# Cross-attention with a mixture-of-experts layer: attention slots and value pieces rearranged, tiles placed on multiples of 128 bytes, the hand-over to the experts changed

## The chip, the cores and the metric

The kernel runs on one core of a Trainium2 chip. The metric is the device time of one execution in microseconds: three runs took 1840.67, 1841.35 and 1837.13 us, median 1840.67. The profiled execution took 1836.25 us.

## The reference, cut to what matters

```python
x = x + tanh(g_xattn) * attention(layernorm(x), ctx, mask)      # x: 8 x 224 x 512, ctx: 8 x 750 x 512
    # Q, K, V = projections, 16 heads of 32; rotary embedding on Q and K
    # softmax(Q K^T / sqrt(32), masked) V, then W_o
xn = layernorm(x)
affinity = softmax(xn @ gate_w.T)                # 8 experts
gating, idx = top_k(affinity per batch and expert, k = 56)
h = silu(x_in @ w_gate) * (x_in @ w_up)          # x_in = xn[idx], 448 rows for each expert, inner width 2048
out.at[idx].add(gating * (h @ w_down))
x = x + tanh(g_ffn) * out
```

Everything is float32. Products that need it are made of three fp32r matmuls (high*high, high*low, low*high), whose low part is the value minus its rounded high part.

## The kernel before, in words

Three stages follow one another, each a block that all engines leave together.

**project_context** makes the keys and values of all 8 batches. `keys` runs 24 matmuls of 376 columns for each group of heads (two column halves n, four slices c of the contraction, three products); `c_hi`, `c_lo` are streamed and `w_hi`, `w_lo` are the weights. `values` does the reverse with 512 columns.

**attend** is written out for 8 batches b and in each for 16 slots t, one for each head. The order is fixed by hand: each engine's `body` has its own list by slot, and semaphores tie the lists. In slot t TensorE turns the softmax numerators of head t (`turn_rows`, three tiles of four transposes from `sm` into the two banks `t_ps`; tile n waits until tile n-2 has been copied out), and makes the scores of head t + 3 (`scores`, two row halves, four matmuls). VectorE masks the scores of head t + 3 (`mask_scores`, two instructions), ScalarE exponentiates those of head t + 2 (`exp`, two instructions). The three tiles are copied to `e_t` by either engine (`empty`); `DVE_TILES` says which go to VectorE. Four heads are a quad. The product with the values (`values`) runs for the quad before, four heads side by side in 32 columns of the array each, in three pieces of two chunks of keys, one piece in each slot with t % 4 not zero, behind the first tile. Other work hangs on slots: the next batch's queries (`turn_x`, `project_q`), the last batch's output projection, layer norm and gate logits (`project_out`, `turn_x2`, `logits`). Softmax sums pass through `invert` (VectorE), `spread_parts` (GpSimd), `turn_parts` (TensorE), `copy_parts` (ScalarE) to `normalise` (VectorE). In `end` the last batch is finished, and `rounds` on VectorE picks the top 56 of 224.

SP's queue carries all plain loads. In `end` it loads the first four tiles of expert weights `w_raw` as soon as the last scores are made.

**experts** loops over 8 experts. A weight tile (128x1024) is loaded to `w_raw`, split by ScalarE (`w_hi`) and VectorE (`w_lo`). `gate_up` runs 24 matmuls for each of 16 tiles (streamed `xs_hi`, `xs_lo`), `down` 24 for each of 8 tiles (streamed `h_hi`, `h_lo`), all with 448 columns. Before the first expert: TensorE brings gates and indices into PSUM (`turned`), VectorE casts the indices (`idx_t`), GpSimd copies one expert's to `gather_i` and issues four gathers of 112 rows into `xg`, TensorE turns them once all four have landed, and ScalarE and VectorE split them (`split_x`). VectorE's and ScalarE's splits of the first three weight tiles stand between the indices and `split_x`.

The start addresses in a partition, modulo 128 bytes, as the allocation gives them:

| tile | before | after |
|---|---|---|
| `xs_hi`, `xs_lo`, `h_lo` (streamed) | 0 | 0 |
| `h_hi` (streamed) | 64 | 0 |
| `ws_hi`, `ws_lo` (expert weights) | 64 | 0 |
| `c_hi`, `c_lo` (streamed in `keys`) | 32, slice pitch 3008 | 0, slice pitch 3072 |
| `w_hi`, `w_lo` (weights in `keys`) | 0 | 0 |
| `ks`, `qs`, `xT`, `e_t` | 64 | 0 |

With the pitch of 3008 and halves that begin 1504 bytes apart, the streamed rows of `keys` in its second half begin at 0, 64, 0, 64 modulo 128 for c = 0 to 3.

Of the kernel before, what the change touches and what calls it, by code (L numbers as in the profile page):

```python
# [7 lines left out]
F32R = mybir.dt.float32r  # L8
# [6 lines left out]
ds = bass.ds  # L15
# [27 lines left out]
LEAD = 3  # L43
WAYS = 32
# [25 lines left out]
F_XT, F_Q, F_USES = 0, 2, 4  # L70

# [46 lines left out]
def program(nc, ctxT, x, maskq, wk, wv, wq, wo, gatew, gx, gf, wstream, consts, rotations, out):  # L118
# [5 lines left out]
    with ExitStack() as top:  # L124
# [15 lines left out]
        w_in = [sem(f"w_in{j}") for j in range(NRAW)]  # L140

        with ExitStack() as mid:
# [8 lines left out]
            with ExitStack() as late:  # L151
                sb(late, "below", [P, IC * SLOTS - E_OVER * (KC // 2) * PAIR])
                w_raw = [sb(late, f"w_raw{j}", [P, UNIT]) for j in range(NRAW)]
# [5 lines left out]
                x_t=sb(mid, "x_t", [QP, QC, D]), xn=sb(mid, "xn", [QP, QC, D]), xT=sb(mid, "xT", [P, 2, 2 * S]),  # L159
                q_rot=sb(mid, "q_rot", [P, NG, S]), q_cos=sb(mid, "q_cos", [P, NG, S]),   # L160
                qs=sb(mid, "qs", [3 * WAYS, H, S], F32R), mq=sb(mid, "mq", [QP, QC, SK]),
                stats=sb(mid, "stats", [QP, QC, 6]), mv=sb(mid, "mv", [QP, 2, QC, 2]), var=sb(mid, "var", [QP, 2, QC]),
                rstd=sb(mid, "rstd", [QP, 2, QC]), minus_half=sb(mid, "minus_half", [QP, QC]), wq=sb(mid, "wq_sb", [P, DC, D]),
# [7 lines left out]

            project_context(nc, sem, sb, ps, both, ctxT, wk, wv, wq, x, maskq, gx, gf, consts, rotations, kd, vd, cst, gains)
            attend(nc, sem, sb, ps, both, x, maskq, wo, gatew, kd, vd, xn_rows, out, cst, ident,
                   cos, sin, gains, gate_all, row_all, wstream, w_raw, w_in)
        experts(nc, sem, sb, ps, w_raw, w_in, wstream, xn_rows, out_rows, cst, ident, gains, gate_all, row_all)


def project_context(nc, sem, sb, ps, both, ctxT, wk, wv, wq, x, maskq, gx, gf, consts, rotations, kd, vd, cst, gains):

    with ExitStack() as st:  # L180
        wraw, c_raw, k_split, v_out = both.wraw, both.c_raw, both.k_split, both.v_out
        w_hi = sb(st, "w_hi", [P, 2, DC, D], F32R)
        w_lo = sb(st, "w_lo", [P, 2, DC, D], F32R)
        graw = sb(st, "graw", [P, 2])
# [3 lines left out]
        c_lo = [sb(st, f"c_lo{j}", [P, DC, SK], F32R) for j in range(2)]  # L188
# [402 lines left out]
VPART = KC // (HG - 1)  # L591
XLEAD = 2
DVE_TILES = {0: (0, 1, 2), 1: (1,), 2: (1,), 6: (1, 2), 7: (0, 1), 8: (0,), 10: (2,), 11: (1,), 12: (1,), 13: (0,), 14: (0,), 15: (1,)}
# [11 lines left out]
def attend(nc, sem, sb, ps, both, x, maskq, wo, gatew, kd, vd, xn_rows, out, cst, ident,  # L605
           cos, sin, gains, gate_all, row_all, wstream, w_raw, w_in):

    with ExitStack() as st:
# [8 lines left out]
        sm = sb(st, "sm", [QP, SR, QC, SK])  # L617
        least, sums = sb(st, "least", [QP, KSLOTS, QC]), sb(st, "sums", [QP, 2, QC, HG])
# [67 lines left out]
        with nc.Block() as block:  # L686
            @block.sync
            def _(sp):
# [63 lines left out]
                def end():  # L752
                    load_res(B - 1)
                    hold(m_made, NS * B)
                    for u in range(NRAW):
                        sp.dma_start(w_raw[u][:], wstream[u]).then_inc(w_in[u], 16)
# [981 lines left out]
```

## Time and profile before

| | us |
|---|---|
| median of three runs | 1840.67 |
| profiled execution | 1836.25 |
| its span, first to last instruction | 1834.4 |
| attention, steady batch | 65.3 |
| last scores to the first expert matmul | 795 to 860.5 |
| experts, from there to the end | 974 |

Columns of the rows below: a timeline row has start, duration, engine, line, operation, `out<-in`, the shape and the count, then how long the engine was idle before it and what ended that. TensorE's matmuls overlap, so how fast they follow is read from one start to the next. A plain fp32 matmul is recorded as two instructions.

### The profile page before, as it was taken

To read this page: it belongs to the slowest core of one execution; us is meant where nothing else is said; L and a number is where in the kernel's file an instruction comes from. 1 tells how busy PE (TensorE), PEld (TensorE's weight loads), DVE (VectorE), ACT (ScalarE), POOL (GpSimd) and SP (SyncE) were. 2 spreads that over 40 slices of the span, in tenths; PEclk is the share of its full clock that TensorE was granted. 3 is DMA by queue.
4 is the path that set the end of the run, shared out by engine and by line. 5 is a ranking of instruction groups with operands and counts; after the bars stand their busy time and mean duration, and the time that the engine had idled before them with its cause. 6 is when DMAs were issued, how large, how long until landed. Compare 5 with 4: busy or idle time off the path is not lost.

```text
span 1834.4 us, 28481 instructions
## 1 busy us (share of the span) xinstructions
PE 1740.8 (95%) x10502; PEld 1545.1 (84%) x10502; DVE 1038.9 (57%) x1786; ACT 839.2 (46%) x1482; POOL 235.4 (13%) x302
## 2 busy tenths in 40 slices
PE   7999999899999999983999999999999999999995
PEld 6898998677777877753999999999999999999995
DVE  6666667777887787754544535435445354453541
ACT  3223225777776877742433434424344243343430
POOL 0000002131231232122000102002020020010101
PEclk9999999999999999995999999999999999999998
DMA  6544547756755755523333535335343252353421
GB/s 242 224 173 186 189 156 220 182 126 153 178 147 135 183 150 134 141 87 96 115 104 103 150 109 143 103 103 151 106 121 127 106 149 104 101 150 109 124 92 20
DMA packets 76301, 251.90 MB, mean 137 GB/s; under 512 B 10784, under 2 KB 10784, under 8 KB 74928
## 3 DMA queue, kind: packets, MB, share of 16 engines
q1 hardware_dynamic: 64208, 216.55, 38.3%
q0 software_dynamic: 12000, 34.12, 7.9%
q8 instruction: 57, 0.93, 0.2%
q14 instruction: 36, 0.29, 0.1%
HBM read 188.01 MB, written 51.61 MB: 131 GB/s over the span
## 4 chain that ended last, share of the span: by engine, by line
PE 52%; POOL 1%; DVE 0%; issue 0%; DMA 0%; DVEq 0%; ACT 0%; POOLq 0%
PE gu_ps L1624 11%; PE gu_ps L1623 11%; PE gu_ps L1622 11%; PE y_ps L1641 6%; PE y_ps L1640 6%; PE y_ps L1639 6%; PE y_ps L1650 1%; PE gu_ps L1608 1%; POOL out L1482 0%; DMA xg<-xn_rows,gather_i 0%; POOL gather_i L1469 0%; POOL xg L1472 0%; DVE xs_lo L1557 0%; DVE y_cols L1584 0%; PE gu_ps L1668 0%
## 5 line engine op out<-in xcount | busy, mean ns | idle before, releaser
L1622 PE MATMUL gu_ps<-xs_hi,ws_hi 128*128 128x448 f32 x1024 | 370.3, 362 | 3.0 <-DVE xs_lo L1557 3.0
L1624 PE MATMUL gu_ps<-xs_hi,ws_lo 128*128 128x448 f32 x1024 | 371.9, 363 | 0.0
L1623 PE MATMUL gu_ps<-xs_lo,ws_hi 128*128 128x448 f32 x1024 | 371.8, 363 | 0.0
L1552 DVE TENSOR_TENSOR ws_lo<-w_raw,ws_hi 128x1024 fp32r<-128x1024 f32 x192 | 235.2, 1226 | 189.3 <-ACT ws_hi L1502 188.3
L1502 ACT ACTIVATE ws_hi<-w_raw 128x1024 fp32r<-128x1024 f32 x192 | 201.5, 1051 | 163.7 <-PE y_ps L1641 150.6
L1298 PEld LDWEIGHTS t_ps<-cst,sm 112*125 112x125 f32 x1536 | 205.0, 190 | 68.6 <-issue 29.3
L990 DVE CUSTOM_DVE_ANT_0 sm<-m_ps,mq 112x752 f32<-112x752 f32 x256 | 229.7, 935 | 34.2 <-PE m_ps L1282 33.8
L1298 PE MATMUL t_ps<-cst,sm 112*125 112x112 f32 x1536 | 233.3, 281 | 15.0 <-DVE e_t L998 11.3
L880 ACT ACTIVATE sm<-sm,least 112x752 f32<-112x752 f32 x256 | 234.7, 919 | 13.7 <-DVE least L990 12.7
L1622 PEld LDWEIGHTS gu_ps<-xs_hi,ws_hi 128*128 128x128 f32 x1024 | 192.0, 187 | 16.9 <-issue 3.3
L1623 PEld LDWEIGHTS gu_ps<-xs_lo,ws_hi 128*128 128x128 f32 x1024 | 192.7, 188 | 14.6
L1624 PEld LDWEIGHTS gu_ps<-xs_hi,ws_lo 128*128 128x128 f32 x1024 | 192.6, 188 | 10.4
L1523 ACT ACTIVATE silu<-gu_ps 128x448 f32<-128x448 f32 x128 | 69.8, 545 | 274.2 <-PE gu_ps L1624 272.2
L1641 PE MATMUL y_ps<-h_hi,ws_lo 128*128 128x448 f32 x512 | 187.8, 367 | 0.0
L1640 PE MATMUL y_ps<-h_lo,ws_hi 128*128 128x448 f32 x512 | 187.6, 367 | 0.0
L1639 PE MATMUL y_ps<-h_hi,ws_hi 128*128 128x448 f32 x512 | 187.4, 366 | 0.0
L887 ACT ACTIVATE e_t<-t_ps 125x448 f32<-125x448 f32 x256 | 137.4, 543 | 107.6 <-PE t_ps L1298 106.2
L1571 DVE TENSOR_TENSOR hid<-silu,gu_ps 128x448 f32<-128x448 f32 x128 | 79.6, 622 | 188.2 <-ACT silu L1523 188.2
L1482 POOL DMA_INDIRECT out<-y_sb,scatter_i x32 | 52.4, 1637 | 860.5 <-DVE y_sb L1562 853.2
L1574 DVE TENSOR_TENSOR h_lo<-hid,h_hi 128x448 fp32r<-128x448 f32 x128 | 80.0, 625 | 82.5 <-ACT h_hi L1525 81.8
L1282 PE MATMUL m_ps<-ks,qs 96*112 96x376 f32 x512 | 120.0, 355 | 5.0 <-PEq L227 1.7
L1525 ACT ACTIVATE h_hi<-hid 128x448 fp32r<-128x448 f32 x128 | 74.0, 578 | 88.0 <-DVE hid L1571 88.0
(153 smaller groups left out, 2438.6 us busy)
## 6 DMA issues: line engine op xcount, KB each, us to landing
w_raw<-wstream SPq DMA_DIRECT2D x192, 512.0 KB, 3.5
ks<-k_split SPq DMA_DIRECT2D x192, 188.0 KB, 5.4
k_split<-k_split SPq DMA_DIRECT2D x32, 752.0 KB, 3.4
v_rows<-v_out SPq DMA_DIRECT2D x16, 750.0 KB
vs<-v_rows SPq DMA_DIRECT2D x16, 750.0 KB
c_raw<-ctxT SPq DMA_DIRECT2D x7, 1500.0 KB, 13.0
qs<-q_hi POOLq DMA_DIRECT2D x64, 112.0 KB, 5.1
mq_raw<-maskq SPq DMA_DIRECT2D x7, 656.2 KB, 10.9
```

What stands on the lines that cost most here:

```text
L880: nc.scalar.activation(rows, rows, ACT.Exp, bias=least[:, h % KSLOTS, qc:qc + 1], scale=-1.0, accum_out=sums[:, h // HG % 2, qc, h % HG:h ...
L887: nc.scalar.activation(e_t[h % (2 * HG)][:, pc], t_ps[tile_of(b, h, pc) % 2][0:KP, 0:PAIR], ACT.Copy).then_inc(t_act, 1)
L990: nc.vector.tensor_tensor_reduce(sm[:, h % SR, qc].rearrange("p (a n) -> p a n", a=2), m_ps[qc][0:QP, :, 0:KN], mq[:, qc].rearrange("p (a ...
L1298: mm = nc.tensor.transpose(t_ps[n % 2][0:KP, a:a + QP], sm[:, h % SR, qc, c * KP:c * KP + KP], ident[0:QP, 0:QP])
L1502: nc.scalar.activation(w_hi[s][:], w_raw[s][:], ACT.Copy).then_inc(whi_done, 1)
L1552: nc.vector.tensor_tensor(w_lo[s][:], w_raw[s][:], w_hi[s][:], ALU.subtract).then_inc(wlo_done[s], 1)
L1622: nc.tensor.matmul(o, w_hi[s][:, w], xs_hi[:, c], start=(c == 0), stop=False)
L1623: nc.tensor.matmul(o, w_hi[s][:, w], xs_lo[:, c], start=False, stop=False)
L1624: mm = nc.tensor.matmul(o, w_lo[s][:, w], xs_hi[:, c], start=False, stop=(c == DC - 1))
L1639: nc.tensor.matmul(o, w_hi[s][:, w], h_hi[:, i], start=(i == 0), stop=False)
L1640: nc.tensor.matmul(o, w_hi[s][:, w], h_lo[:, i], start=False, stop=False)
L1641: mm = nc.tensor.matmul(o, w_lo[s][:, w], h_hi[:, i], start=False, stop=(i == IC - 1))
```

## The change

In `attend`, the three value pieces of a quad become one or two, put at the end of a slot: all six chunks in slots 1 and 7, four and two in 10 and 11, four and two in 13 and 15. The four score matmuls of a slot are parted, two ahead of tile 1 and two behind it. ScalarE makes both exponentials behind tile 0. `DVE_TILES` gives VectorE 15 tiles of 48 and not 16, in other slots. Most side work moves by a slot or two. The copies of the weight tiles to `w_hi` and `w_lo` for the first three units move from the start of `experts` to the end of `attend`.

In `experts`, VectorE writes `gather_i` for expert 0 straight from PSUM, ahead of the gates; each of the four gathers has its own semaphore, TensorE turns each when it has landed, the first matmuls wait for `xs_lo` slice by slice, and SP loads nothing further until the first gathers have landed. Tiles are moved and padded as in the table above.

```diff
-DVE_TILES = {0: (0, 1, 2), 1: (1,), 2: (1,), 6: (1, 2), 7: (0, 1), 8: (0,), 10: (2,), 11: (1,), 12: (1,), 13: (0,), 14: (0,), 15: (1,)}
+V_CHUNKS = {1: (0, KC), 7: (0, KC), 10: (0, 4), 11: (4, KC), 13: (0, 4), 15: (4, KC)}
+DVE_TILES = {0: (0,), 1: (0, 1), 2: (1,), 3: (1,), 4: (0, 1), 6: (1,), 8: (0,), 9: (1,), 11: (0, 1), 12: (0,), 14: (1,), 15: (0,)}
...
-        c_hi = [sb(st, f"c_hi{j}", [P, DC, SK], F32R) for j in range(2)]
+        c_hi = [sb(st, f"c_hi{j}", [P, DC, SK + LINE // 2], F32R) for j in range(2)]
...
# attend, ScalarE
-                            if pc < QC:
-                                next_exp(pc)
+                            if pc == 0:
+                                for qc in range(QC):
+                                    next_exp(qc)
...
                 def end():
                     copy_parts(B - 1, NG - 1)
+                    for u in range(LEAD):
+                        act.wait_ge(first.w_in[u], 16)
+                        nc.scalar.activation(first.w_hi[u][:], first.w_raw[u][:], ACT.Copy).then_inc(first.whi_done, 1)
                     x2_columns(B - 1, 0)
...
# attend, VectorE, end
                     norm_2(b)
+                    low_w(0)
                     dve.wait_ge(rest_made, R_USES * b + R_XNT + 2)
                     nc.vector.tensor_copy(xT[:, 1], m_ps[1][:, 1, 0:2 * S]).then_inc(rest_free, 1)
+                    low_w(1)
+                    low_w(2)
                     logits(b)
...
# attend, TensorE, a slot
                         turn_rows(b, t, 0)
-                        if t % HG:
-                            last_values()
+                        next_scores(0)
                         turn_rows(b, t, 1)
-                        next_scores(0)
                         next_scores(1)
                         turn_rows(b, t, 2)
...
+                        if t in V_CHUNKS:
+                            last_values()
...
# attend, TensorE, end
-                    for part in range(HG - 1):
-                        values(b, NG - 1, part)
+                    values(b, NG - 1, (0, KC))
...
# experts, SP
+                for g in range(RG):
+                    hold(gathered[g], 16)
                 for u in range(NRAW, NU):
                     load(0, u)
...
# experts, GpSimd
+                    if isinstance(e, int) and e == 0:
+                        hold(gidx_done, 1)
...
# experts, VectorE
                 dve.wait_ge(turned, 1)
+                nc.vector.tensor_copy(gather_i, gu_ps[0][0:RP, RG * E:2 * RG * E].rearrange("p (g e) -> p g e", g=RG)[:, :, 0:1]
+                                      .rearrange("p g o -> p (g o)")).then_inc(gidx_done, 1)
...
-                for u in range(LEAD):
-                    split_w(0, u)
                 split_x(0)
...
# experts, TensorE
-                    pe.wait_ge(gathered, 16 * RG * (e + 1))
-                    for c in range(DC):
-                        for g in range(RG):
+                    for g in range(RG):
+                        pe.wait_ge(gathered[g], 16 * (e + 1))
+                        for c in range(DC):
...
-                    if u == 0:
-                        pe.wait_ge(xlo_done, DC * (e + 1))
...
+                            if u == 0 and k == 0:
+                                pe.wait_ge(xlo_done, DC * e + c + 1)
```

TensorE's instructions in program order, slot 7 of a middle batch, before. `t_ps` are the transposes, `m_ps` the scores, `o_ps<-e_t,vs` a piece of values, `w_ps<-wo_sb,cx` the output projection; a count is of matmuls in the program, and the piece stands behind the first tile.

```order
L1298 MATMUL t_ps<-cst,sm 125x112 x4
L1322 MATMUL o_ps<-e_t,vs 32x224 x8
L1298 MATMUL t_ps<-cst,sm 125x112 x4
L1282 MATMUL m_ps<-ks,qs 112x376 x4
L1298 MATMUL t_ps<-cst,sm 125x112 x4
L1222 MATMUL w_ps<-wo_sb,cx 112x512 x2
```

The same slot in the changed kernel:

```order
L1330 MATMUL t_ps<-cst,sm 125x112 x4
L1314 MATMUL m_ps<-ks,qs 112x376 x2
L1330 MATMUL t_ps<-cst,sm 125x112 x4
L1314 MATMUL m_ps<-ks,qs 112x376 x2
L1330 MATMUL t_ps<-cst,sm 125x112 x4
L1254 MATMUL w_ps<-wo_sb,cx 112x512 x2
L1354 MATMUL o_ps<-e_t,vs 32x224 x24
```

Slots 5 and 6 have lost their pieces of 8, one piece of 24 closes slot 7, and the scores are parted.

VectorE from the last layer norm to the gate logits, at the end of `attend`, after the change (`ws_lo` are low parts of the first weight tiles, `lg` the logits):

```order
L999 TENSOR_SCALAR xn<-x_res,mv,rstd 112x512 x2
L1121 TENSOR_TENSOR ws_lo<-w_raw,ws_hi 128x1024
L1207 COPY xT<-m_ps 128x448
L1121 TENSOR_TENSOR ws_lo<-w_raw,ws_hi 128x1024 x2
L1085 COPY lg<-w_ps 112x16
```

VectorE from the end of `attend` into `experts`, before the change; the three `ws_lo` stand behind the indices and ahead of the split of the gathered rows:

```order
L1089 TENSOR_SCALAR gate_all<-top_v,cst 64x56
L1090 TENSOR_SCALAR row_all<-top_i,cst 64x56
L686 UNCONDITIONAL_BRANCH
L1547 UNCONDITIONAL_BRANCH
L1588 TENSOR_SCALAR gate_t<-gu_ps,gains 112x4x8
L1590 CAST idx_t<-gu_ps 112x4x8
L1552 TENSOR_TENSOR ws_lo<-w_raw,ws_hi 128x1024 x3
L1557 TENSOR_TENSOR xs_lo<-gu_ps,xs_hi 128x448 x4
```

And after; the index copy of expert 0 (`both_i` holds `gather_i`) has come from GpSimd and is first:

```order
L1113 TENSOR_SCALAR gate_all<-top_v,cst 64x56
L1114 TENSOR_SCALAR row_all<-top_i,cst 64x56
L706 UNCONDITIONAL_BRANCH
L1580 UNCONDITIONAL_BRANCH
L1621 CAST both_i<-gu_ps 112x4
L1623 TENSOR_SCALAR gate_t<-gu_ps,gains 112x4x8
L1625 CAST idx_t<-gu_ps 112x4x8
L1590 TENSOR_TENSOR xs_lo<-gu_ps,xs_hi 128x448 x4
```

Nothing of VectorE's own stands between the indices and the split any more.

## Rows read from the trace of the kernel before

**Rows 1.** Busy time by stage: us, then PE, PEld, DVE, ACT, POOL, clock, DMA.

```profile
540.10:605.40 65.30, 62.65 (x538) 50.44 (x537) 52.14 (x125) 48.82 (x108) 17.07 (x27) 1.00 0.65 155
800.00:850.00 50.00, 22.54 (x168) 14.79 (x168) 22.71 (x75) 7.87 (x15) 11.92 (x11) 0.69 0.30 102
```

**Rows 2.** Timeline of TensorE in the last batch, a piece of values among others.

```profile
771.33 0.59 PE L1298 MATMUL t_ps<-cst,sm 112*125 112x112 f32 x4
771.85 0.96 PE L1322 MATMUL o_ps<-e_t,vs 125*32 125x224 f32 x16
...
773.20 0.92 PE L1282 MATMUL m_ps<-ks,qs 96*112 96x376 f32 x4
...
780.88 1.02 PE L1298 MATMUL t_ps<-cst,sm 112*125 112x112 f32 x8
...
781.67 0.91 PE L1282 MATMUL m_ps<-ks,qs 96*112 96x376 f32 x4
...
811.73 2.48 PE L1322 MATMUL o_ps<-e_t,vs 125*32 125x224 f32 x48
```

**Rows 3.** Waits of TensorE in three steady batches: total, times, longest.

```profile
PE t_ps L1298 <- DVE e_t L998: 4.2, 6, 0.8
```

**Rows 4.** Instruction groups in one steady batch: busy us, mean ns, idle before.

```profile
L880 ACT ACTIVATE sm<-sm,least 112x752 f32<-112x752 f32 x34 | 31.2, 920 | 1.2 <-DVE least L990 1.1
L990 DVE CUSTOM_DVE_ANT_0 sm<-m_ps,mq 112x752 f32<-112x752 f32 x33 | 29.6, 934 | 3.7 <-PE m_ps L1282 3.7
...
L887 ACT ACTIVATE e_t<-t_ps 125x448 f32<-125x448 f32 x32 | 17.3, 544 | 14.1 <-PE t_ps L1298 13.9
```

**Rows 5.** Timeline at the end of `attend`, last batch's gate logits.

```profile
809.02 1.86 SPq L756 DMA_DIRECT2D w_raw<-wstream  x4
...
822.79 0.54 ACT L857 ACTIVATE xT<-w_ps 128x448 f32<-128x448 f32 x1 [12.32 <-PE w_ps L1249]
823.09 3.11 POOL L795 TENSOR_SCALAR x2o<-x_res,flags_sb 112x512 f32<-112x512 f32 x2
823.17 0.62 DVE L1177 COPY xT<-m_ps 128x448 f32<-128x448 f32 x1 [1.46 <-PE m_ps L1249]
...
827.04 0.17 DVE L1061 COPY lg<-w_ps 112x16 f32<-112x16 f32 x1 [3.25 <-PE w_ps L1262]
```

**Rows 6.** Timeline at the start of `experts`, VectorE and GpSimd.

```profile
842.28 3.48 DVE L1552 TENSOR_TENSOR ws_lo<-w_raw,ws_hi 128x1024 fp32r<-128x1024 f32 x3
842.47 3.35 POOL L1469 COPY gather_i<-idx_t 112x4 uint32<-112x4 uint32 x1 [14.97 <-DVE idx_t L1590]
```

**Rows 7.** Chain of waits that ended last, in order of time: start, us, what.

```profile
846.71 1.05 POOL xg L1472
...
850.55 3.58 DMA xg<-xn_rows,gather_i
854.27 3.23 PE gu_ps L1608 x16
...
858.11 2.23 DVE xs_lo L1557 x4
860.47 0.71 PE gu_ps L1622
861.18 0.37 PE gu_ps L1623
```

**Rows 8.** Lines of the expert matmuls in 880:930 and 950:974: min/median/max ns, first and last start.

```profile
L1622 PE MATMUL gu_ps<-xs_hi,ws_hi x84: 360/360/360, 880.0 to 929.8; 128*128 128x448 f32 x84
...
L1639 PE MATMUL y_ps<-h_hi,ws_hi x40: 362/364/450, 950.1 to 974.0; 128*128 128x448 f32 x40
```

**Rows 9.** Timeline of `keys`, second half, first matmul of slices c = 0 to 2.

```profile
242.15 0.33 PE L526 MATMUL k_ps<-c_hi,w_hi 128*128 128x376 f32 x1
...
242.67 0.33 PE L526 MATMUL k_ps<-c_hi,w_hi 128*128 128x376 f32 x1
...
243.18 0.33 PE L526 MATMUL k_ps<-c_hi,w_hi 128*128 128x376 f32 x1
```

More of the change, by code:

```diff
@@ L43 @@
 LEAD = 3
+LINE = 32
+TOP_EDGE, MID_EDGE = 16, 16
+BEFORE = 2 * (B // 2) * D + DC * SLOTS + 2 * SLOTS
+FIRST = BEFORE + 3 * LINE
 WAYS = 32
@@ L70 @@
 F_XT, F_Q, F_USES = 0, 2, 4
+@dataclass
+class First:
+    w_raw: object
+    w_hi: object
+    w_lo: object
+    w_in: object
+    whi_done: object
+    wlo_done: object
 @dataclass
@@ L139, in program @@
         gains = sb(top, "gains", [P, 2])
-        w_in = [sem(f"w_in{j}") for j in range(NRAW)]
+        sb(top, "top_edge", [P, TOP_EDGE])
         with ExitStack() as mid:
@@ L151, in program @@
             with ExitStack() as late:
-                sb(late, "below", [P, IC * SLOTS - E_OVER * (KC // 2) * PAIR])
-                w_raw = [sb(late, f"w_raw{j}", [P, UNIT]) for j in range(NRAW)]
+                sb(late, "below", [P, FIRST - E_OVER * (KC // 2) * PAIR])
+                first = First(
+                    w_raw=[sb(late, f"w_raw{j}", [P, UNIT]) for j in range(NRAW)],
+                    w_hi=[sb(late, f"ws_hi{j}", [P, UNIT], F32R) for j in range(NRAW)],
+                    w_lo=[sb(late, f"ws_lo{j}", [P, UNIT], F32R) for j in range(NRAW)],
+                    w_in=[sem(f"w_in{j}") for j in range(NRAW)], whi_done=sem("whi_done"),
+                    wlo_done=[sem(f"wlo_done{j}") for j in range(NRAW)])
             ks = sb(mid, "ks", [3 * WAYS, KSLOTS, SK], F32R)
@@ L183, in project_context @@
         w_lo = sb(st, "w_lo", [P, 2, DC, D], F32R)
+        c_hi = [sb(st, f"c_hi{j}", [P, DC, SK + LINE // 2], F32R) for j in range(2)]
+        c_lo = [sb(st, f"c_lo{j}", [P, DC, SK + LINE // 2], F32R) for j in range(2)]
         graw = sb(st, "graw", [P, 2])
@@ L605, in attend @@
 def attend(nc, sem, sb, ps, both, x, maskq, wo, gatew, kd, vd, xn_rows, out, cst, ident,
[L606 removed]
+           cos, sin, gains, gate_all, row_all, wstream, first):
     with ExitStack() as st:
@@ L617, in attend @@
         sm = sb(st, "sm", [QP, SR, QC, SK])
+        e_t = [sb(st, f"e_t{j}", [KP, KC // 2, PAIR]) for j in range(E_OVER, 2 * HG)] + both.e_t
         least, sums = sb(st, "least", [QP, KSLOTS, QC]), sb(st, "sums", [QP, 2, QC, HG])
         parts, spread = sb(st, "parts", [QP, 2, QC * HG]), sb(st, "spread", [QP, 2, QC, P])
-        e_t = [sb(st, f"e_t{j}", [KP, KC // 2, PAIR]) for j in range(E_OVER, 2 * HG)] + both.e_t
         c_r, cx = sb(st, "c_r", [P, S]), sb(st, "cx", [P, NG, S])
@@ L1092, in _, with low_w @@
                 SOFT = 4
+                def low_w(u):
+                    dve.wait_ge(first.whi_done, u + 1)
+                    nc.vector.tensor_tensor(first.w_lo[u][:], first.w_raw[u][:], first.w_hi[u][:], ALU.subtract).then_inc(first.wlo_done[u], 1)
                 def start():
@@ L1307, in turn_parts, with values @@
                     mm.then_inc(r_made, 1)
-                def values(b, q, part):
+                def values(b, q, chunks):
                     a, quad = q // 2, q % 2
-                    if part == 0:
+                    if chunks[0] == 0:
                         if quad == 0:
@@ L1317, in values @@
                             pe.wait_ge(s_, v_)
-                    for c in range(VPART * part, VPART * part + VPART):
+                    for c in range(*chunks):
                         for r in range(HG):
@@ L1423, in experts @@
         gidx_done, sidx_done = sem("gidx_done"), sem("sidx_done")
-        gathered, x_turned, xhi_done, xlo_done = sem("gathered"), sem("x_turned"), sem("xhi_done"), sem("xlo_done")
+        gathered, x_turned, xhi_done, xlo_done = [sem(f"gathered{g}") for g in range(RG)], sem("x_turned"), sem("xhi_done"), sem("xlo_done")
         silu_done, hid_done = sem("silu_done"), [sem(f"hid_done{j}") for j in range(2)]
@@ L1591, in _ @@
                                       gu_ps[0][0:RP, RG * E:2 * RG * E].rearrange("p (g e) -> p g e", g=RG)).then_inc(idx_ready, 1)
-                for u in range(LEAD):
-                    split_w(0, u)
                 split_x(0)
```

123 lines of the change are left out of this document (61 added, 62 removed).

## The prediction

> **What bounds the kernel now.** I read the busy time by stage first, then the timeline of each stage, the waits and the chain. In a steady batch of the attention TensorE is busy for 62.65 of 65.3 us, VectorE for 52.1, ScalarE for 48.8; between the attention and the experts TensorE works for less than half of 50 us, at a mean clock of 0.69 [rows 1]. In the attention TensorE sets the pace, and its 2.65 us of idle time in a batch are short waits for a copy out of `t_ps` [rows 3]. In the gap everything is one chain: last layer norm, gate logits, top-k on VectorE, indices, gathers, transposes, split, first matmul at 860.47 [rows 5 to 7]. From there TensorE has work without a break to the end. So the change is read at three places: the attention's slots, the gap, and the pace of the matmuls.
>
> **The attention's slots: fewer pieces.** Four transposes, a piece of 16 instructions (8 matmuls) and four transposes take from 771.33 to 773.20, 1.87 us; eight transposes with no piece between them take from 780.88 to 781.67, 0.79 us [rows 2]. A piece costs 1.08 us. The last quad's single piece of 48 takes 2.48 us [rows 2]; three of 16 would be 3.24. So each piece that is left out saves (3.24 - 2.48) / 2 = 0.38 us; since the end of a matmul is modelled I take 0.35. Before there are 9 pieces in the first batch, 12 in each of seven, and one at the end: 94. Now 5, 6 each, and one: 48. Of the 46 saved, the 4 of batch 0 count for nothing, because that batch has no output projection and its copies hold it anyway. 42 x 0.35 = **-14.7 us**.
>
> Parting the scores costs nothing that I can find: the four matmuls and their neighbours are the same, and one more change between transposes and scores replaces one that was there beside a piece. Bounds: 0, or, if each change costs what a piece's edges do beyond its work (0.35), 128 slots x 0.35 = +45. The second is far off, as eight transposes with scores behind them show no such gap [rows 2]; I take 0 and +4 as its end. It also gives each tile more time to be copied out, which could take away waits.
>
> What is late next: the pieces no longer fill every slot. A slot with neither piece nor projection holds 12 transposes and four scores, some 2.1 us of TensorE (0.79 + 0.4 + 0.9 [rows 2]), but ScalarE needs two exponentials of 0.92 and two or three copies of 0.54, 2.9 to 3.5 us [rows 4]. Such slots were 0, 8 and 12; now they are 0, 8, 9 and 12. In slots 0, 8, 9, 12 ScalarE's lists come to 3.8, 3.3, 2.9 and 3.3 us (with the copies of sums and `xT`), TensorE's to 2.65, 2.25, 2.4 and 2.25 (small transposes included): 3.7 us of waits in a batch, if nothing is carried over from slot to slot. But exponentials run two heads ahead, and in slots 5 to 7, where TensorE has an output projection or six chunks on top of its 2.1 us, the others catch up. The same reckoning for the old order gives about 4 (with VectorE's three copies in slot 0), where 2.65 were idle. I take the waits as unchanged: 0, between -1.3 us a batch (half of them go, as a piece no longer waits for `copy_parts` in slots 9 and 13) and +1.05 (3.7 against 2.65): -10 to +8 in all.
>
> **The end of the attention.** In the last batch the last piece of quad 2 now ends slot 15, right ahead of `turn_parts`, which needs its `normalise`: one exposed multiply and its hand-over, **+0.6**. ScalarE's three copies of weights: it has been idle for 12.32 us at 822.79, the loads are issued at 809.02 to 810.9, and three copies of 1 us fit: 0 [rows 5]. VectorE's first `ws_lo` (1.16 us: three in 3.48 [rows 6]) follows the layer norm, which ends at 821.7, and the copy to `xT` before began at 823.17: hidden but for nothing to spare. The other two, 2.3 us, follow that copy, 823.8 to 826.1, and the logits' copy comes at 827.04: hidden [rows 5]. But GpSimd's `x2o` runs from 823.09 for 3.11 us [rows 5]. In rows 6 a small GpSimd copy of 16 numbers lasts 3.35 us, exactly as long as VectorE's three `ws_lo` beside it. If here VectorE is the one that waits, for each of two instructions of 1.55 us, the logits' copy slips to about 828.7. So 0 to +1.6; I take **+0.5**.
>
> The Trainium skill says on this, in "SBUF — State Buffer", section "Who interferes with whom", that a VectorE instruction with two SBUF inputs and a GpSimd instruction that reads SBUF exclude each other for the whole instruction, and whichever comes first blocks the other. By that rule the trace agrees with its 3.35 us, and both ends of this term and the gain of the next one follow from it.
>
> **The start of the experts.** GpSimd's copy of indices (842.47, 3.35 us) goes. The cast on VectorE at 842.02 lasts 0.2, and the same 0.85 us lie from its end to the first gather (845.8 to 846.71): it is issued at 843.15, **-3.55** [rows 6, 7]. Four gathers follow at the same spacing; the last lands at 854.13 - 3.55 = 850.6 [rows 7]. All 16 transposes were behind it, 3.23 us; now 12 are done, and four are left, 0.8 us: **-2.4**. The first matmul waited for all four `xs_lo` (2.23 us), now for the first, 0.56: **-1.7** [rows 7]. A slice's matmuls at the low clock take three times 0.37 us and a split 0.56, so the later slices aren't waited for. Sum -7.65. Three loads of 0.5 MB no longer share the time of the gathers; worth nothing to -0.5. Against it, TensorE may spend longer at the low of its two clocks (1.2 of 2.4 GHz): now some nine matmuls at 0.37 for 0.20, which is 1.5 us; twice that is the end. The gap in all: -7.65 + 0.6 + 0.5 = **-6.5**, -8.5 to -3.5.
>
> **The pace of the fp32r matmuls.** `gate_up`, streaming at 0 modulo 128 with weights at 64: 84 of one line from 880.0 to 929.8, three lines in turn, 49.8 / 249 = 0.200 us. `down`, where two of three stream `h_hi` at 64: 23.9 / 117 = 0.204 [rows 8]. If the offset makes the difference, aligning wins 0.004 x 1536 = 6 us. In `keys` the weights are at 0; slice c = 0 streams at 0 and takes 0.52 us for three matmuls of 376, slice c = 1 at 64 and takes 0.51 [rows 9]. There, alignment shows no gain at all. The 0.004 may as well come from `down` changing its accumulator every three matmuls. For `keys`, `values` and `scores`, 1856 matmuls, I allow 0 to -5 by the same spread of 0.003. On the other side, where both streams begin at 0 the slice was 0.01 slower; 0.003 x 3072 matmuls of `gate_up` would be +9. The bounds are +9 and -11; I take **-5**, nearest to the row of `down`.
>
> The Trainium skill's page "SBUF — State Buffer", section "Specifications (TRN2)", gives lines of 16 bytes. All offsets here were multiples of 32, so by that rule this term is 0 and the sum 5 us less gain; rows 9 agree with it, rows 8 leave it open.
>
> **Sum.** 1836.25 - 14.7 - 6.5 - 5 = 1810.0 for a profiled execution. The three runs of before lie 1 to 5 us above the profiled one, their median 4.4; I add 3: **1813 us**.
>
> **Rivals.** (a) The attention gives the gain back: 3.7 us of waits in a batch for 2.65, +8, and dearer changes between scores and tiles, +4: -2.7 in the attention, 1825 to 1829. For it speak ScalarE's full short slots, against it that its total is 48.8 of 65.3 [rows 1]. (b) Slower than before: no slot hides another's excess. Then VectorE's slot 4 (two masks 1.87, two copies 1.24, `normalise`, and the rotation and sum of the queries, of some 2.5: 5.9 us against TensorE's 3.8) and slot 13 (+0.7) join the 3.7: 6.5 us of waits in place of 2.65, +31 in eight batches, with no gain from alignment: 1836.25 - 14.7 - 6.5 + 31 = 1846, as a median 1849. It decides from 3.4 us of further waits in a batch. Against it: the old order by the same count would have idled for more than 6. (c) The offsets rule the matmul: at the low clock a matmul of 448 columns takes 0.37 us, twice 0.187, while at the high clock it takes 0.200 [rows 7, 8]. If full alignment removed that 0.0135 from 4608 matmuls, -62: about 1755. Against it rows 9, though 376 columns are no multiple of 32. The Trainium skill ("TensorE: Matmul & The Clock Gate", section "Wait — 56ns, not 53.3ns?") has 2.5 ns over the columns' own time for bf16, 0.189 here; by that it would be -51. No fp32r row of this trace reaches it. (d) Streams and weights at the same offset hinder one another: +9 for -5, 1827.
>
> **Chances.** Within 0.3% (5.5 us) of before can't be told from no change. Forecast 0.63; (a) 0.18; (b) 0.07; (c) 0.05; (d) 0.07. The forecast, (c), most of (a) and (d) are faster: 0.87; what spills over from (a), (b) and (d) into no change 0.07; slower 0.06. The forecast's own range is 1800 to 1824. With (a) and (d) taken in, 1798 to 1831; (b) and (c) lie outside.
>
> **What would show it.** Steady batches of about 63.4 us with 6 groups of value instructions; PE's idle time near 2.65 in each. If it exceeds 3.7, (a). First gather about 1.2 us after the index matmuls end at 841.97, not 4.7; transposes in four groups; first expert matmul some 12 us after those matmuls begin and not 19. `down` at 0.200 and `gate_up` still at 0.200. The forecast is wrong if the batch stays at 65, or if either pace moves by more than 0.004.

## The result and the profile after

The changed kernel takes 1846.14 us, median of 7 runs (1842.28 to 1855.62), against 1839.95 for the kernel before in 7 runs beside it (1837.13 to 1842.3): ratio of the runs 1.0047, interval 1.0032 to 1.0062 (the two medians alone give 1.0034). It is slower by a third to half a per cent; 1813 us had been forecast, and 1846 lies outside the range. The profiled execution took 1842.28 us with a span of 1840.5.

The starts of instructions in both traces cut the span into stages. The last two columns are for the version that the experiments lead to.

| stage, from and to | before | after | difference | e9_best |
|---|---|---|---|---|
| up to the first transpose of the attention | 295.7 | 296.4 | +0.7 | 296.5 |
| to the last transpose of a head's rows | 512.2 | 505.9 | -6.3 | 472.6 |
| to the first `gate_up` matmul | 52.6 | 47.1 | -5.5 | 47.3 |
| to the last `down` matmul | 951.9 | 968.8 | +16.9 | 947.0 |

The attention and the gap got shorter, the experts longer by more than both.

**The attention.** Two steady batches and the 50 us at the end of the attention, as [rows 1] (us, then busy time of PE, PEld, DVE, ACT, POOL, the granted clock, DMA):

```profile
482.90:547.10 64.20, 61.66 (x540) 51.09 (x536) 52.32 (x123) 48.60 (x108) 16.32 (x26) 0.97 0.65 157
547.15:611.90 64.75, 61.76 (x541) 51.04 (x537) 52.37 (x124) 48.69 (x108) 16.33 (x26) 0.97 0.68 160
...
800.00:850.00 50.00, 21.77 (x139) 13.71 (x138) 23.31 (x74) 7.01 (x14) 11.18 (x12) 0.67 0.28 94
```

From first transpose to first transpose the batches 1 to 6 take 64.0, 64.5, 64.3, 64.7, 64.8 and 65.3 us, so that none is more than 1.3 us shorter than the 65.3 of a steady batch before. What is new is the clock: 0.97, where [rows 1] has 1.00. TensorE's waits in three steady batches, as [rows 3]:

```profile
PE m_ps L1314 <- issue: 8.3, 3, 2.9
```

All the waits for a copy out of `t_ps` are gone, and one new wait stands in their place, once in each batch. "issue" says that no engine's work ended it. The timeline shows it in slot 1, ahead of the first scores of head 4 (start, us, engine, line, what):

```profile
549.78 0.60 PE L1330 MATMUL t_ps<-cst,sm 112*125 112x112 f32 x4
...
550.13 0.08 DVE L1014 DVE_READ_ACCUMULATOR2_ANT least<- 112x1 f32 x1
...
553.28 0.57 PE L1314 MATMUL m_ps<-ks,qs 96*112 96x376 f32 x2 [2.89 <-issue]
```

The mask of the head before was done at 550.2, so `m_ps` was free. Each DMA lands in 16 shares, and the trace records when: the last of the 48 shares of the keys for heads 4 and 5 landed at 553.19. The same batch cut at the wait, same columns:

```profile
547.15:550.40 3.25, 3.24 (x30) 3.06 (x26) 2.73 (x7) 3.09 (x8) 0.00 (x0) 1.00 1.04 227
550.40:553.25 2.85, 0.00 (x0) 0.00 (x1) 0.62 (x1) 2.03 (x5) 0.00 (x0) 1.00 1.05 227
553.25:555.00 1.75, 1.72 (x14) 1.75 (x15) 0.69 (x2) 0.00 (x0) 0.00 (x0) 1.00 1.04 159
555.00:558.40 3.40, 3.40 (x37) 1.86 (x39) 1.76 (x5) 1.09 (x2) 0.00 (x0) 0.51 1.01 205
558.40:611.90 53.50, 53.40 (x471) 44.37 (x461) 46.56 (x110) 42.48 (x94) 16.33 (x26) 1.00 0.60 150
```

Behind the 2.85 us without work the granted clock goes to 0.51, which is 1.2 of 2.4 GHz, for 3.4 us in which TensorE is busy throughout. That is another 1.7 us. The DMA shares of 1.01 to 1.05 say that the DMA engines are full up to 558.4. So the wait costs some 4.7 us in this batch, and without it the batch would be 60.0. Over the whole attention it is seven such waits, in the batches 1 to 7:

```profile
PE m_ps L1314 <- issue: 19.0, 7, 3.3
```

Six of them, in the batches 1 to 6, have 3.4 us at half the clock behind them. The one in batch 7, 2.43 us long, has not; a seventh such stretch begins at 797.4, 50 us behind it.

**The gap.** The end of the attention, as [rows 5], and the chain at the start of the experts, as [rows 6, 7]:

```profile
817.71 1.22 DVE L1121 TENSOR_TENSOR ws_lo<-w_raw,ws_hi 128x1024 fp32r<-128x1024 f32 x1
...
818.92 0.62 DVE L1207 COPY xT<-m_ps 128x448 f32<-128x448 f32 x1
819.17 4.26 POOL L815 TENSOR_SCALAR x2o<-x_res,flags_sb 112x512 f32<-112x512 f32 x2
819.46 2.63 DVE L1121 TENSOR_TENSOR ws_lo<-w_raw,ws_hi 128x1024 fp32r<-128x1024 f32 x2
...
822.79 0.17 DVE L1085 COPY lg<-w_ps 112x16 f32<-112x16 f32 x1 [0.70 <-PE w_ps L1294]
```

```profile
836.90 0.94 PE gu_ps L1701 x4
838.08 0.85 issue
838.93 1.04 POOL xg L1508
...
841.52 4.76 DMA xg<-xn_rows,both_i
846.33 1.77 PE gu_ps L1641 x8
848.13 0.55 ACT xs_hi L1542
848.70 0.64 DVE xs_lo L1590
849.47 0.71 PE gu_ps L1655
```

The logits' copy stands 3.87 us behind the start of the copy to `xT`, as before (823.17 to 827.04 in [rows 5]): the splits of weights hide there. GpSimd's `x2o` took 4.26 instead of 3.11 us, which nobody waits for. The first gather starts 1.1 us after the index matmuls' end, the first expert matmul 12.6 us after their start.

**The experts.** `gate_up` at 1000 to 1040 and 1120 to 1160, then `down` at 950 to 974, as [rows 8]; the first row is of before in the same stretch:

```profile
L1622 PE MATMUL gu_ps<-xs_hi,ws_hi x67: 360/360/360, 999.8 to 1039.4; 128*128 128x448 f32 x67
```

```profile
L1655 PE MATMUL gu_ps<-xs_hi,ws_hi x67: 362/365/369, 999.6 to 1039.8; 128*128 128x448 f32 x67
...
L1655 PE MATMUL gu_ps<-xs_hi,ws_hi x65: 368/368/368, 1120.0 to 1159.6; 128*128 128x448 f32 x65
...
L1672 PE MATMUL y_ps<-h_hi,ws_hi x37: 368/368/368, 949.8 to 972.2; 128*128 128x448 f32 x37
```

Before: 39.6 us for 66 x 3 matmuls, 0.200 us each. After: 40.2 for as many, 0.203, and in the second stretch 39.6 for 64 x 3, 0.206. Taken from start to start, the pace in the changed kernel is locked, that is, it stays at one value over hundreds of matmuls: 202.7 ns in one expert, 206.7 in the next, in turn, with `down` like `gate_up`. It changes within the first 96 matmuls of an expert. The means are 204.7 and 204.6 where before had 200.0 and 203.7. Over 3072 and 1536 matmuls that is 14.4 + 1.4 us, nearly all of the 16.9.

In `keys`, where [rows 9] had 0.52 and 0.51 us for three matmuls, both differences between the three starts are now 0.52. Over the whole stage the mean is 173.2 ns for 172.1, and that of `values` 232.6 for 232.1, about 1 us in all:

```profile
241.85 0.33 PE L546 MATMUL k_ps<-c_hi,w_hi 128*128 128x376 f32 x1
...
242.37 0.34 PE L546 MATMUL k_ps<-c_hi,w_hi 128*128 128x376 f32 x1
...
242.89 0.34 PE L546 MATMUL k_ps<-c_hi,w_hi 128*128 128x376 f32 x1
```

### The profile page after: what moved, and what is told of

Read it like the earlier page. It is cut to its first block, busy times and chain, and to the rows that moved or that the text cites. A ratio compares the mean times of both kernels' runs of the same rounds, so it can differ in the third digit from the quotient of the medians.

```text
span 1840.5 us, 28531 instructions
## 1 busy us (share of the span) xinstructions
PE 1753.1 (95%) x10502; PEld 1553.2 (84%) x10502; DVE 1040.7 (57%) x1779; ACT 837.8 (46%) x1490; POOL 226.6 (12%) x301
## 4 chain that ended last, share of the span: by engine, by line
PE 53%; POOL 0%; DMA 0%; issue 0%; DVE 0%; DVEq 0%; ACT 0%; POOLq 0%
PE gu_ps L1655 11%; PE gu_ps L1656 11%; PE gu_ps L1657 11%; PE y_ps L1672 6%; PE y_ps L1673 6%; PE y_ps L1674 6%; PE y_ps L1683 1%; PE gu_ps L1641 1%; POOL out L1518 0%; DMA xg<-xn_rows,both_i 0%; POOL xg L1508 0%; DVE y_cols L1617 0%; PE gu_ps L1701 0%; DVE y_sb L1595 0%; DVEq L1466 0%
## 5 line engine op out<-in xcount | busy, mean ns | idle before, releaser
L1655 PE MATMUL gu_ps<-xs_hi,ws_hi 128*128 128x448 f32 x1024 | 377.3, 368 | 1.4 <-DVE xs_lo L1590 1.4
L1657 PE MATMUL gu_ps<-xs_hi,ws_lo 128*128 128x448 f32 x1024 | 376.5, 368 | 0.0
L1656 PE MATMUL gu_ps<-xs_lo,ws_hi 128*128 128x448 f32 x1024 | 376.4, 368 | 0.0
L1330 PEld LDWEIGHTS t_ps<-cst,sm 112*125 112x125 f32 x1536 | 218.5, 190 | 31.8 <-issue 26.8
L1314 PE MATMUL m_ps<-ks,qs 96*112 96x376 f32 x512 | 150.7, 377 | 24.9 <-issue 19.0
L1518 POOL DMA_INDIRECT out<-y_sb,both_i x32 | 53.1, 1659 | 877.7 <-DVE y_sb L1595 870.4
```

What stands on the lines that cost most here:

```text
L1314: mm = nc.tensor.matmul(m_ps[qc][0:QP, n, 0:KN], qs[:, h, qc * QP:qc * QP + QP], ks[:, h % KSLOTS, n * KN:n * KN + KN], start=True, stop=True)
L1330: mm = nc.tensor.transpose(t_ps[n % 2][0:KP, a:a + QP], sm[:, h % SR, qc, c * KP:c * KP + KP], ident[0:QP, 0:QP])
L1655: nc.tensor.matmul(o, w_hi[s][:, w], xs_hi[:, c], start=(c == 0), stop=False)
L1656: nc.tensor.matmul(o, w_hi[s][:, w], xs_lo[:, c], start=False, stop=False)
L1657: mm = nc.tensor.matmul(o, w_lo[s][:, w], xs_hi[:, c], start=False, stop=(c == DC - 1))
```

## The experiments

Theory: two things cost what the rest gains. One is that streams and weights of the experts now start at the same offset modulo 128 bytes (before: `xs` 0, `h_hi` 64, `h_lo` 0, weights 64; now all 0). The other is the keys of head 4, which land late behind the values. Ratios are against the kernel before, which ran beside each; paces are means from start to start.

**e1_weights64.** The weights alone go back to 64.

```
-FIRST = BEFORE + 3 * LINE
+FIRST = BEFORE + 3 * LINE + LINE // 2
...
-        sb(st, "first_place", [P, 3 * NRAW, UNIT])
+        sb(st, "first_gap", [P, LINE // 2]), sb(st, "first_place", [P, 3 * NRAW, UNIT]), sb(st, "stream_gap", [P, LINE // 2])
```

> The changed kernel with the experts' weights (raw, high and low parts) 64 bytes further on, so that they start at 64 mod 128 as in the kernel before, while every streamed tile (xs, h) stays at 0. Theory 1 (a streamed row and the next weights at one offset mod 128 hinder one another): gate_up falls from 204.7 back to 200.0 ns a matmul (3072 of them, -14.4 us) and down, whose high part now differs from the weights too, from 204.6 to 200.0 (1536, -7.1 us): about 1825 us against 1846. Theory 2 (the slower pace comes from something else in the new build, such as where its code or its other tiles lie): both stay near 204.7 and the time stays within 3 us of 1846. Theory 3 (only the streams' own alignment counts, 200 wherever they are at 0): already refuted by the changed kernel unless the weights' offset matters, so it expects no change either.

Measured: 1823.75 us, ratio 0.9915 (0.9884 to 0.9946). `gate_up` and `down` both at 200.0 in every stretch. Theory 1 holds to the number, and `down` is faster than in either kernel.

```profile
L1655 PE MATMUL gu_ps<-xs_hi,ws_hi x67: 360/360/360, 1000.2 to 1039.8; 128*128 128x448 f32 x67
```

**e4_before0.** The converse: in the kernel before, everything of the experts at 0.

```
-                sb(late, "below", [P, IC * SLOTS - E_OVER * (KC // 2) * PAIR])
+                sb(late, "below", [P, 16 + IC * SLOTS - E_OVER * (KC // 2) * PAIR])
...
-        h_hi = sb(st, "h_hi", [P, IC, SLOTS], F32R)
+        sb(st, "gap", [P, 16]); h_hi = sb(st, "h_hi", [P, IC, SLOTS], F32R)
...
-        xg = sb(st, "xg", [RP, RG, D])
+        sb(st, "gap2", [P, 16]); xg = sb(st, "xg", [RP, RG, D])
```

> The kernel before with the experts' weights and the high part of h moved by 64 bytes, so that weights and streams all start at 0 mod 128 as in the changed kernel; nothing else is changed. Theory 1 (equal offsets hinder): gate_up slows from 200.0 to about 204.7 ns (+14.4 us), down goes from 203.7 to about 204.6 (+1.4): about 1855 us against 1840. Theory 2 (another part of the change made it): the pace stays 200.0 and 203.7 and the time within 3 us of 1840.

Measured: 1850.63 us, ratio 1.0065 (1.0048 to 1.0082), +12. `gate_up` 204.0, `down` 203.4. So 64 bytes more under the weights, with nothing else of the change, make the kernel before slow in the same way. (`h_hi` moves along by 64 bytes and `xs` by 128, which leaves `xs` at 0.) Here the pace is the same in every expert, another lock than that of the changed kernel.

**e2_map, e7_w32, e8_all64.** What about the other distances? In the first, buffer j of the weights starts at 32j (`UNIT + 8` wide) and chunk c of a stream at 32c (`SLOTS + 8` wide). The second is e1_weights64 with 8 floats ahead of the weights and 24 behind them instead of 16 and 16, the third e1_weights64 without `stream_gap`.

> One look for the pace alone. The four weight buffers of the experts start at 0, 32, 64 and 96 mod 128 (high and low part alike), and chunk c of the streamed tiles starts at 32c mod 128, so that each pair of offsets occurs in every expert. Theory 1 (equal offsets hinder): matmuls whose stream and weights have one offset take about 204.7 ns from start to start, those 64 bytes apart 200.0, with the quarter turns between or like one of the two. Theory 3 (a stream off a 128-byte line costs by itself): pace goes by the chunk alone, chunks 1 and 3 slowest. Theory 2 (neither): all combinations within 1 ns of each other. If the pace locks over a whole stretch, as the changed kernel's does (206.7 and 202.7 in turn from expert to expert), single combinations will not differ and only the stretch's mean will.

> One look for the pace: as the kernel with the weights at 64, but the weights at 32 mod 128 with the streams at 0. If what hinders is that both start in the same half of a 128-byte line, gate_up and down take more than 202 ns here; if only the very same offset does, 200.0; if 64 bytes apart is a special case, between 201 and 206, as the map of all pairs had (203.9 and 203.5).

> One look for the pace: weights and streams (xs, h) all at 64 mod 128. If the distance between the two is what counts, gate_up and down are as slow as with both at 0 (202.6 to 206.7, mean about 204.6); if a start at 64 of the weights by itself is what makes them fast, 200.0.

Measured, one execution each (1841.93, 1847.12, 1836.75 us), so that only the paces are compared:

| kernel | streams, weights (mod 128) | `gate_up`, ns | `down`, ns |
|---|---|---|---|
| before | `xs` 0, `h_hi` 64, `h_lo` 0; 64 | 200.0 | 203.7 |
| after | 0; 0 | 204.7 (202.7 or 206.7) | 204.6 |
| e4_before0 | 0; 0 | 204.0 | 203.4 |
| e8_all64 | 64; 64 | 203.2 (202.7 or 206.7) | 202.8 |
| e7_w32 | 0; 32 | 205.3 | 205.3 |
| e2_map | all pairs | 203.9 | 203.5 |
| e1_weights64 | 0; 64 | 200.0 | 200.0 |

The distance counts, not the offset itself: both at 64 is as slow, and locks at the same two paces, as both at 0. A distance of 32 is no better. Only 64 apart gives 200.0. The map did not tell single pairs apart: its pace too is locked over whole stretches, so that a pair's matmul depends on its neighbours. It shows only that a mixture isn't fast. No run moves one of the two operands by 128 bytes alone, so that the distance repeats every 128 bytes is how the offsets are written here and not shown.

**e3_keys.** The values are loaded behind the keys of heads 4 and 5.

```
-                        if t == 12 and not last:
+                        if t == 14 and not last:
                             load_v(b + 1, 0)
```

> The changed kernel with one DMA moved: the values of the next batch (750 KB) are loaded by SP behind the keys of its heads 4 and 5 instead of ahead of them (slot 14 of SP's order instead of 12). Theory A (the new 3.1 us wait of slot 1, at the first scores of head 4, is for keys that queue behind the values): the keys land 4 us or more earlier, the wait goes in the 6 or 7 batches that have it, about -18 us of the attention (ends 2 to 3 us a batch earlier), time about 1828. Theory B (the 16 DMA engines are saturated in this stretch whatever the order): the keys land at most 1 us earlier, the wait stays over 2 us, and the time within 6 us of 1846. Theory C (what is late next takes the place): the wait at head 4 goes, but another of over 1.5 us a batch shows in slots 2 to 7, for ACT's exp or head 6's keys.

Measured: 1814.97 us, ratio 0.9857 (0.9837 to 0.9877), 31 us less than the changed kernel, where 18 were expected. The keys of head 4 land 13.5 us ahead of the batch's first transpose, where they landed 6.0 after it. The wait is gone in all seven batches and nothing takes its place: a batch is 60.0 us. What I had left out was the clock: with the wait its half-speed stretch goes too. In batch 0 two waits of 3.6 and 3.8 us appeared, which end at 321.2 and 339.1 us, as keys land. The attention takes 482.5 us with them and 472.4 in the next version, which doesn't have them.

**e5_split.** The order stays, but the values are two DMAs.

```
-                    sp.dma_start(vs[a][:]..., vd[ds(b, 1), a]...).then_inc(vs_in[a], 16)
+                    for r in (slice(0, 112), slice(112, KP)):
+                        sp.dma_start(vs[a][r]..., vd[ds(b, 1), a, r]...).then_inc(vs_in[a], 16)
...
-                            pe.wait_ge(vs_in[a], 16 * b + 16)
+                            pe.wait_ge(vs_in[a], 32 * b + 32)
```

> The changed kernel with the order of its loads untouched, but each value load (125 rows, 750 KB) issued as two DMAs, of 112 and of 13 rows. In the trace of the changed kernel only 5 of the 16 shares of such a load land late (12 to 14 us after its issue, the other shares at once), and of the 16 shares of the keys for head 4 behind it 11 land within 7 us and 5 only after those. Theory A1 (125 rows are dealt out to 5 of the 16 DMA engines, and the keys' shares on those 5 wait behind them): with 112 rows dealt to 16, the keys of head 4 land before slot 1 although they still stand behind the values, the wait goes and the time falls to about 1815 to 1820, as where the keys were put first. Theory A2 (what counts is the 750 KB ahead of the keys, on whatever engines): the keys land less than 2 us earlier, the wait stays over 1.5 us a batch and the time stays above 1835.

Measured: 1806.81 us, ratio 0.9823 (0.9807 to 0.9839). Theory A1 holds: the keys still stand behind 750 KB and land in time. The landings of one batch's shares, in us from the issue of the values:

```
                      values: first, last         keys of heads 4 and 5: 33rd share, 34th, 48th
after (issued 534.75) 0.5; 5 shares at 13.1-14.1  7.0, 15.0, 18.4
e5_split (520.39)     1.0; 5.3                    7.1, 7.1, 7.9
```

A load of keys is three DMAs of 16 shares. In the changed kernel 33 shares, three times 11, are there after 7.0 us; the other 15, three times 5, come from 15.0 on, behind the 5 late shares of the values. Which engine carried a share isn't in the traces; that it is 11 engines and 5 is read from the counts. 125 rows have no larger divisor up to 16 than 5, while 112 go to all 16. The Trainium skill states this rule in "DMA: Bandwidth & Descriptors", section "Why a DMA increments its semaphore by 16 and not by 1": the outermost dimension is dealt to the largest number of engines up to 16 that divides it on both sides of the transfer, source and destination. The traces agree, with 5 late shares of 16.

The row of a whole batch of e5_split, as [rows 1], and the stretch that begins where the changed kernel fell to half speed, 5.0 us of work into the batch:

```profile
532.80:592.80 60.00, 59.90 (x540) 50.40 (x536) 52.39 (x125) 48.49 (x108) 16.34 (x26) 1.00 0.67 170
```

```profile
537.80:541.20 3.40, 3.40 (x57) 2.35 (x56) 1.51 (x5) 1.33 (x5) 0.00 (x0) 1.00 1.00 254
```

TensorE is busy for 59.90 of 60.00 us, and does 57 instructions in 3.4 us where it did 37. The DMA engines are nearly as full as in the changed kernel (1.00 for 1.01 in these rows), and the keys are there all the same: fullness was not what delayed them.

**e12_before_split.** The same edit in the kernel before.

> The kernel before with only its value loads issued as two DMAs (112 and 13 rows). In it the keys of head 4 land 4 us before they are needed, so the theory that says the value loads matter only by that wait expects no gain in the slots: 1838 within 3 us, and the whole 33 us between the changed kernel and its mended form is what the new arrangement of the slots lacked. Rival: the loads on 5 of 16 engines also delay others (stacked queries, mask, x) and the old waits of slots 8, 9, 12 and 13: then 5 us or more faster.

Measured: 1834.98 us, ratio 0.9979 (0.9967 to 0.999). The keys land 5.4 to 6.5 us before the first transpose instead of 0.2 to 1.9 after it, and the steady batches gain nothing: TensorE's waits in three of them are those of [rows 3], to a tenth:

```profile
PE t_ps L1298 <- DVE e_t L998: 4.3, 6, 0.8
```

So the 0.2% is not in the steady slots. One batch of the kernel before was not steady: in batch 1 the keys of heads 4 and 5 landed at 360.36 us, 7.0 after the first transpose. TensorE waited, and then ran at half its clock (a row of the timeline, and one by stage as in [rows 1]):

```profile
360.45 0.92 PE L1282 MATMUL m_ps<-ks,qs 96*112 96x376 f32 x4 [1.60 <-issue]
...
361.90:365.30 3.40, 3.40 (x25) 2.15 (x24) 1.11 (x4) 3.10 (x6) 0.00 (x0) 0.50 0.35 126
```

That batch took 68.2 us for 65.3, and takes 64.8 in e12_before_split. Batch 0 takes 59.5 there for 57.6, with a stretch at half the clock that it didn't have, and the attention as a whole 510.7 for 512.2. So apart from batch 1 the value loads cost something only where the new slots are.

**e11_gap_back and e9_best.** e9_best is the changed kernel with e5_split's and e1_weights64's edits. e11_gap_back is e9_best with the gap as before: splits at the start of `experts`, indices by GpSimd, one wait for all gathers and one for all low parts.

> The changed kernel with the values loaded as two DMAs (112 and 13 rows) and the experts' weights 64 bytes further on; the order of the loads is as in the changed kernel. If the two mendings add: 1806.8 (values in two, weights at 0) - 4608 matmuls x 4.65 ns = 21.4 us: 1785. Rival: the weights' shift costs something elsewhere (it gained 22 us alone but 20.5 beside the moved load, with longer half-clock stretches), then 1788 to 1792. In both cases gate_up and down at 200.0 ns, slots at 60.0 us a batch.

> As e9_best, but the part between attention and experts put back as in the kernel before: the first three weight units are split at the start of the experts, the first gather's indices are cast by GpSimd after all index work, the transposes wait for all four gathers, the first matmul for all four low parts. Nothing else changes, and the pace is locked at 200.0 ns in both. The prediction's own working of this edit: -7.65 us at the start of the experts, +0.6 and +0.5 given back at the end of the attention and on GpSimd: this kernel should take 5 to 8 us more than e9_best (about 1792). Rival: since TensorE's clock is at half speed in this stretch and comes back only some time after the work resumes, the saved idle time comes out otherwise: less than 3 or more than 9 us.

Measured: e9_best 1787.48 us, ratio 0.9719 (0.9706 to 0.9733); e11_gap_back 1794.99, ratio 0.9764 (0.9749 to 0.9779). The edit of the gap is worth 7.5 us; by the traces 54.1 - 47.3 = 6.8. The chain of e11_gap_back has GpSimd's copy of the indices back, 3.36 us where [rows 6] had 3.35:

```profile
804.64 3.36 POOL both_i L1493
```

**e6_both and e10_proj.** e6_both is e3_keys' edit with e1_weights64's. e10_proj is e9_best with the projections' weights 64 bytes further on too (16 floats ahead of `w_hi`, 16 behind `w_lo`).

> The changed kernel with both mendings: the experts' weights 64 bytes further on and the values loaded behind the keys of heads 4 and 5. If the two causes are separate and all of it, the times add: 1846 - 22 (weights moved) - 31 (keys first) = about 1793, with gate_up and down at 200.0 ns and the slots' batch at 60.0 us. Rival: they overlap by way of TensorE's clock (the weights' kernel had three more half-clock stretches in the attention and a 37.5 us one in the gap), then between 1795 and 1805.

> As e9_best, and the high and low weights of the keys' and values' projections 64 bytes further on too, with the context's chunks left at 0. By the rule found in the experts (the pace depends on the distance of stream and weights) the keys (768 matmuls of 376 columns, 173.3 ns) gain where the distance becomes 64: half of them (the second 376 columns start 96 bytes on) and the values (576 of 512 columns, 232.7 ns, their stationary rows start at multiples of 500 bytes) only here and there: 0 to 5 us less than e9_best. Rival: the rule doesn't hold for operands that change their distance from one matmul to the next: no change within 1 us, or keys slower.

Measured: e6_both 1794.45 us, ratio 0.9745 (0.9726 to 0.9763): the two causes add. It has e3_keys' waits in batch 0 too (the attention takes 482.7 us), which is where e9_best, with 472.6, is better. e10_proj 1784.93 us, ratio 0.9716 (0.9702 to 0.9729): `keys` went from 173.2 to 171.5 ns, `values` from 232.6 to 233.3. Together 768 x 1.7 less 576 x 0.6 is 1 us, and the interval is nearly e9_best's: inconclusive as a time.

## Why the prediction was wrong

The profiled execution took 32.3 us more than the 1810.0 forecast for it. By the stages that is 22 from the pace, 33.5 from new waits, 1 from the gap and 0.7 from the start, less 25 that the rest of the attention gained beyond its term. Two steps failed, and nearly half of what they cost was hidden by waits that went although the forecast had kept them.

**The pace of the matmuls, -5 us: the sign was wrong, and it measured +16.9.** This term failed by 22 us. The step that failed is "If the offset makes the difference, aligning wins 0.004 x 1536 = 6 us", from which -5 was taken, "nearest to the row of `down`". The right reading was in the same rows: `gate_up`, with streams and weights 64 apart, was the fast one at 0.200. `down`, two of whose three products have both at 64, was slower at 0.204, and in `keys` the slice with both at 0 took 0.52 for 0.51. I read the rows as ones of alignment, while they were of distance. Rival (d) named the mechanism, "streams and weights at the same offset hinder one another". I gave it 0.07, and priced it by `keys` at 3 ns where it is 4.7. For the bound I trusted a spread of 0.003 between two slices. e1_weights64 and e4_before0 show it in both directions. The reading by which this term is 0, because all offsets are multiples of 32, fell too: 64 bytes are worth 4.7 ns. Rival (c) fell: 200.0 is the floor of all kernels here.

**Waits of the attention, 0: missed a new one, +33.5.** The step that failed is "What is late next": it counts engines slot by slot and not the landings of loads. The same edit that ended the pieces earlier moved the need of head 4's keys from 5.8 us after the batch's first transpose to 3.2, and their landing from 0.2 to 1.9 us after it to 5.2 to 6.5, since the values' load waits for slot 11, now closer to the batch's end. The prediction named each engine that "is late next" and no DMA. A third of the price was then the clock, which the forecast had only in the gap. The seven waits are 19.0 us, one of 1.1 for keys stands in batch 0, and the seven stretches at half the clock cost 11.9: 32 us. The attention of e5_split is 472.4 us long against 505.9, which is the 33.5. The trace of before had the warning: batch 1 already waited 1.60 us there for the same keys and fell to half the clock (e12_before_split). I had read only steady batches.

**The rest of the attention, -14.7: right in its mechanism, and short on the waits.** Without the keys' wait a batch is 60.0 for 65.3. The six pieces fewer are worth 6 x 0.32 = 1.9 a batch (0.35 assumed), counted from start to start, so about -13 in seven batches. Of the other 3.4 us a batch (5.3 - 1.9) 2.55 are the idle time of the old waits, which went from 2.65 to 0.10 and so entirely; 0.8 lie in TensorE's busy time, whose ends are modelled, and were not traced to a cause. Batch by batch, the 39.8 us between 512.2 and 472.4 are -1.4, -8.2 (batch 1, which had waited for keys), five times -5.3, and -3.8 in the last. I had allowed for half of the waits, -10 at best, and set 0. Parting the scores cost nothing that the starts show: in a steady batch four scores with the changes on both sides take 0.82 us before, and 0.94 after, with one change of 0.11 between transposes less. So rival (a) was wrong in its place as well: no short slot idles. Rival (b), slower by VectorE's full slots, gave 1849 and came near the time by luck; its 31 us of waits for VectorE were not there.

**The gap, -6.5: right.** -5.5 in the changed kernel, 6.8 to 7.5 by e11_gap_back. The start of the experts came as worked out. The +0.6 for the exposed multiply is there: `turn_parts` waits 0.52 us for `normalise`. The +0.5 for GpSimd and VectorE measured 0: GpSimd's two instructions took 4.26 us for 3.11 and VectorE's two 2.63 for 2.3, but the logits wait for TensorE (0.70 us in the row above). TensorE was at half speed for 37.5 us around the gap against 44.4, so it didn't stay longer at the low clock.

Sum in the traces: +0.7 - 6.3 - 5.5 + 16.9 = +5.8. What the forecast saw of the change was there; with its two faults mended the kernel takes 1787 us, 26 less than the forecast.

Open: why a distance of 32 is as slow as none, and why the same offsets lock at different paces from expert to expert in one build and not in another. The seven runs of the changed kernel lie 13 us apart, those of e9_best 1.6. The lock isn't what makes this spread: e1_weights64, at 200.0 throughout, spreads by 13 us too, and e5_split, whose pace is locked as in the changed kernel, by 3.4. The spread is wide where TensorE waits for keys (8.1 and 9.7 us in e3_keys and e6_both) and narrow where it doesn't, but how a wait makes it was not shown.

## What to carry to other kernels

Before a change that shortens the work between a load's trigger and its use, list the landings of the loads as well as the engines' busy time: the time from landing to use is the reserve, and here it was 4 us. Look at the first batches as well as at the steady ones: one of them had no reserve left. A DMA over a number of rows with only small divisors fills a few engines, and whatever is queued behind it arrives with the slowest of them; splitting off the odd rows is one line. When tiles are moved to "aligned" addresses, look at the distance between the two operands of the busiest matmuls, in a trace from start to start, before and after.

## What was not expected of the hardware

- The pace of fp32r matmuls of 448 columns in a row depends on the distance modulo 128 bytes between the streamed tile and the weights: 200.0 ns at 64, 202.7 to 206.7 at 0, 205.3 at 32. The pace locks over hundreds of matmuls, in some builds over all of them.
- The Trainium skill, "SBUF — State Buffer", section "Who interferes with whom", says that TensorE never waits on anyone for SBUF. As to the other engines no run here speaks against it, but its own pace depends on how its two operands lie to one another, by up to 6.7 ns in 200. That their two reads hold one another up is the likely reason, and was not shown.
- A wait of 2.85 us cost 1.7 us more by the granted clock (0.51 for 3.4 us), and so did one of 1.60 in batch 1 of the kernel before. One of 2.43 us in batch 7 of the changed kernel did not, nor did the waits of up to 0.8 us of the kernel before [rows 3].
- A 750 KB load over 125 rows took 14 us, with 5 of its 16 shares late, and 5.3 us as 112 and 13 rows.
